# A grouped convolution in the mixed form a second time, and z copied out of PSUM before it is split

## The reference

```python
x = x + conv(x, w0, groups=4, 9 taps, padding 4) + (cond @ c_w0.T + side)[:, :, None]
x = x + agg_w1 @ x + agg_b1[:, :, None]     # agg_w = sum_k att_k W_k, att = softmax of a small MLP of cond
x = x + agg_w2 @ x + agg_b2[:, :, None]
x = x + conv(x, w3, groups=4, 9 taps, padding 4) + (cond @ c_w3.T + side)[:, :, None]
```

## Time and profile before

| | us |
|---|---|
| median of 3 runs | 632.01 (631.92 to 632.13) |
| the profiled execution | 635.33 |
| its span, first to last instruction | 633.5 |
| TensorE busy (share of the span) | 622.8 (98%) |
| VectorE busy | 500.9 (79%) |
| ScalarE busy | 338.2 (53%) |
| GpSimd busy | 272.3 (43%) |
| mean granted TensorE clock | 0.991 |

### The profile page before, as it was taken

One profiled execution on the slowest core, in us unless ns is written; L12 is line 12 of the kernel. 1 busy time (PEld: TensorE's weight loads), 2 busy tenths in 40 slices (PEclk: granted clock), 3 DMA queues, 4 the chain that ended last, 5 costly groups with the idle time before them and its releaser, 6 DMA issues.

```text
span 633.5 us, 26750 instructions
## 1 busy us (share of the span) xinstructions
PE 622.8 (98%) x11938; PEld 506.3 (80%) x11938; DVE 500.9 (79%) x1002; ACT 338.2 (53%) x626; POOL 272.3 (43%) x163
## 2 busy tenths in 40 slices
PE   8999999999999999999999999999999999999995
PEld 6888897777788777889877778777878877788874
DVE  6899777978777887887887887797877788788735
ACT  4665455555455456455456446555545545645534
POOL 4133454354355345355435345435435534534220
PEclk8999999999999999999999999999999999999998
DMA  8066665557765556775555776555776555655515
GB/s 244 24 188 215 203 211 177 204 163 225 232 207 156 190 176 199 232 232 158 173 191 175 232 232 182 158 202 162 223 232 208 155 190 176 201 169 168 161 76 201
DMA packets 50572, 118.84 MB, mean 188 GB/s; under 512 B 5621, under 2 KB 26282, under 8 KB 42714
## 3 DMA queue, kind: packets, MB, share of 16 engines
q1 hardware_dynamic: 49170, 116.04, 58.1%
q0 software_dynamic: 576, 1.26, 0.5%
q10 hardware_dynamic: 776, 0.89, 0.4%
HBM read 35.33 MB, written 33.55 MB: 109 GB/s over the span
## 4 chain that ended last, share of the span: by engine, by line
PE 96%; DMA 2%; DVE 1%; ACT 1%; issue 0%; ACTq 0%; DVEq 0%
PE ps L1068 45%; PE ps L1079 19%; PE ps L1090 16%; PE ps L1214 14%; PE ps L1192 1%; DMA out_sb<-in_L_cond_weight 1%; DMA out_planes<-out_taps 1%; ACT out_sb L740 1%; PE ps L1262 0%; PE ps L1185 0%; DVE out_taps L856 0%; DVE x_in L950 0%; DVE x_hi L993 0%; PE ps L1250 0%; PE ps L1302 0%
## 5 line engine op out<-in xcount | busy, mean ns | idle before, releaser
L513 POOL COPY out_sb<-out_planes 128x2048 f32<-128x2048 f32 x30 | 123.0, 4099 | 187.8 <-issue 162.0
L496 POOL COPY x_full<-x_in 128x2048 f32<-128x2048 f32 x29 | 117.1, 4038 | 113.9 <-DVE x_lo L822 110.1
L846 DVE SCALAR_TENSOR_TENSOR z_lo<-ps,bias_tab,z_hi 128x1024 fp32r<-128x1024 f32 x62 | 76.7, 1279 | 60.7 <-ACT z_hi L649 60.7
L1090 PE MATMUL ps<-x_full,taps_raw 32*32 32x512 f32 x2880 | 102.2, 598 | 0.0
L1068 PEld LDWEIGHTS ps<-z_hi,taps_hi 32*128 32x128 f32 x1488 | 71.0, 183 | 35.4 <-issue 25.1
L1068 PE MATMUL ps<-z_hi,taps_lo 32*128 32x512 f32 x1488 | 96.5, 387 | 0.0
L836 DVE SCALAR_TENSOR_TENSOR y_lo<-ps,bias_tab,y_hi 128x512 fp32r<-128x512 f32 x128 | 87.2, 744 | 10.2 <-ACT y_hi L639 10.2
L1068 PE MATMUL ps<-z_hi,taps_hi 32*128 32x512 f32 x1488 | 94.2, 396 | 0.0
L657 ACT ACTIVATE out_taps<-ps,bias_tab 128x512 f32<-128x512 f32 x62 | 39.3, 685 | 102.2 <-PE ps L1068 102.2
L1068 PE MATMUL ps<-z_lo,taps_hi 32*128 32x512 f32 x1488 | 90.3, 385 | 0.0
L1214 PE MATMUL ps<-y_hi,mix_w 32*128 32x512 f32 x1024 | 88.0, 385 | 0.0
(11 more groups left out here) (158 smaller groups left out, 831.0 us busy)
## 6 DMA issues: line engine op xcount, KB each, us to landing
x_in<-in_x SPq DMA_DIRECT2D x31, 1024.0 KB, 5.3
out_planes<-out_taps SPq DMA_DIRECT2D x122, 256.0 KB, 3.6
out<-out_sb SPq DMA_DIRECT2D x30, 1024.0 KB, 4.6
mix_w<-prod SPq DMA_DIRECT2D x124, 128.0 KB, 4.0
x_in<-in_x SPq DMA_DIRECT2D x2, 512.0 KB, 5.9
out<-out_sb POOLq DMA_DIRECT2D x2, 512.0 KB, 3.5
out<-x_full SPq DMA_DIRECT2D x7, 128.0 KB, 2.9
out_taps<-in_L_cond_weight SPq DMA_DIRECT2D x1, 512.0 KB, 5.8
```

The lines of the kernel that those rows point to most:

```text
L496: pool.tensor_copy(row_order(t, d, x[:, :, home(t, d)]), x_order(t, d, x_in[t.par(d)][:, :])).then_inc(x_planed, 1)
L513: pool.tensor_copy(x_order(t, d, out_sb[t.par(d)][:, :]), row_order(t, d, out_planes[:, :, :]))\
L846: dve.scalar_tensor_tensor(out=z_home(t, 0)[1][:, 2 * h:2 * h + 2, home(t, 0)], in0=ps[:, k:k + 2, :], scalar=bias_tab[:, b, 2 * G:BIAS], ...
L1090: tile = pe.matmul(ps[rows(p), first_bank + g, :], taps_raw[l][rows(g), d - p, :], full[rows(g), d % PH, c:c + S], start=False, stop=(n == ...
```

## The change

Conv3 of tiles 1 to 30 takes the mixed form too. Step t now runs conv0 of tile t with its three tile rounds last, then directly conv3 of tile t - 1 with its three tile rounds first, so that the six stand together, then 6 whole rounds, the product (or, in the last step, the mix), and 12 whole rounds; then the mix. The tile rounds need z unsplit, so ScalarE writes z with its bias from PSUM to a new buffer `z_full` in two halves, fills z_full's edges, and then makes z_hi from z_full in one copy; VectorE makes z_lo from z_full and z_hi in one operation. Conv3's tile rounds wait for z_lo_done and z_full's edges.

The output columns of conv3's weights are now ordered as conv0's, by phase and then by channel, so `relay_out` reads 32 neighbouring partitions for each phase instead of every fourth. The last tile keeps the old order: its taps are made again in conv0's weight buffers (GpSimd clears them after the last conv0, ScalarE and VectorE fill them), and its biases come in a small `bias_last` by four DMA transfers in step 16.

```diff
+FIRST_FULL_Z = 1
+        def full_z(t, d):
+            return not isinstance(t.half, int) or FIRST_FULL_Z <= t.i + d < N - 1
...
-                    sp.dma_start(out_planes[:, p, :], out_taps[p:C:PH, :, :]).then_inc(out_relaid, DMA)
+                    sp.dma_start(out_planes[:, p, :], out_taps[rows(p), :, :]).then_inc(out_relaid, DMA)
...
+            def bias_for_last():
+                pool.wait_ge(bias_tab_done, 3)
+                for p in range(PH):
+                    pool.dma_start(bias_last[p:C:PH, :], bias_tab[rows(p), N - 1, G:2 * G]).then_inc(bias_last_in, DMA)
+            def zero_last_taps():
+                pool.wait_ge(conv0_done, G * N)
+                for w in (taps_hi[0], taps_lo[0]):
+                    pool.memset(w[:, :, :].bitcast(F32), 0.0).then_inc(last_taps_zeroed, 1)
...
-                    for o, i in edges(z):
+                    for o, i in (edges(z, slice(PH - 1, PH), slice(0, 1)) if full_z(t, 0) else edges(z)):
...
+            def whole_z(t):                       # called by high_z(t) where full_z(t, 0)
+                b = t.i
+                for h in range(2):
+                    act.wait_ge(mix_done, PH * b + 2 * h + 2)
+                    k = bank(t, 0) + 2 * h
+                    act.activation(z_full[:, 2 * h:2 * h + 2, home(t, 0)], ps[:, k:k + 2, :], ACT.Identity,
+                                   bias=bias_tab[:, b, 2 * G:BIAS]).then_inc(z_full_done, 1)
+                act.wait_ge(z_full_done, 2 * (b + 1 - FIRST_FULL_Z))
+                for o, i in full_edges(z_full):
+                    last = act.activation(o, i, ACT.Copy)
+                last.then_inc(z_full_edged, 1)
+                act.activation(z_hi[:, :, home(t, 0)], z_full[:, :, home(t, 0)], ACT.Copy).then_inc(z_hi_done, 2)
...
+            def last_taps_high():                 # ScalarE, step 31, ahead of high_z; VectorE has last_taps_low
+                act.wait_ge(last_taps_zeroed, 2)
+                for p in range(PH):
+                    act.activation(last_columns(taps_hi, p), taps_raw[1][:, :, :], ACT.Copy).then_inc(last_taps_hi_done, 1)
...
             def low_z(t):
                 b = t.i
+                if full_z(t, 0):
+                    dve.wait_ge(z_hi_done, 2 * (b + 1))
+                    dve.tensor_tensor(out=z_lo[:, :, home(t, 0)], in0=z_full[:, :, home(t, 0)],
+                                      in1=z_hi[:, :, home(t, 0)].bitcast(F32), op=ALU.subtract).then_inc(z_lo_done, 2)
+                    return
...
+            def conv3_mixed(t, turns, middle):
+                b = t.i - 1
+                order = [(k, d) for k in range(2) for d in WHOLE] + [(2, d) for d in WHOLE]
+                if t.at(2):
+                    pe.wait_ge(taps_raw_step[1], 2)
+                    pe.wait_ge(prod_summed, b + 2)
+                pe.wait_ge(z_lo_done, 2 * (b + 1))
+                pe.wait_ge(z_full_edged, b + 1 - FIRST_FULL_Z)
+                pe.nop(nofuse=True)
+                partial_turns(bank(t, -1), 1, z_full, BLK, first=True)
+                pe.wait_ge(z_edged, b + 1 - PLAIN)
+                whole_turns(bank(t, -1), 1, z_hi, z_lo, order[:turns], BLK)
+                middle()
+                whole_turns(bank(t, -1), 1, z_hi, z_lo, order[turns:], BLK, done=conv3_done)
...
-            LATER = 20
+            LATER = 6
...
-                mid = MID + 4 if t.at(2) else MID if t.at(N - 1) else LATER
-                if t.has(-1):
-                    conv3(t, -1, range(mid))
-                if t.has(1):
-                    product(t, 1)
...
+                elif t.at(N - 1):
+                    conv3_mixed(t, LATER, lambda: mix(t))
+                else:
+                    conv3_mixed(t, LATER, lambda: product(t, 1))
                     mix(t)
```

More of the change, by code:

```diff
@@ L580, in _ @@
                 pool.memset(buf[:, :, ROW - 1:ROW].bitcast(F32), 0.0).then_inc(far_zeroed, 1)
-            for buf in x_full:
+            for buf in x_full + [z_full]:
                 pool.memset(buf[:, :, 0:ROW:ROW - 1], 0.0).then_inc(far_zeroed, 1)
@@ L592, in conditioned_residual_kernel @@
         HALOS = 6
-        FAR = 8
+        FAR = 9
         @block.scalar
@@ L940, in one, with last_taps_low @@
                     low_z(t)
+            def last_taps_low():
+                dve.wait_ge(last_taps_zeroed, 2)
+                for p in range(PH):
+                    dve.wait_ge(last_taps_hi_done, p + 1)
+                    dve.tensor_tensor(out=last_columns(taps_lo, p), in0=taps_raw[1][:, :, :],
+                                      in1=last_columns(taps_hi, p).bitcast(F32), op=ALU.subtract)\
+                       .then_inc(last_taps_lo_done, 1)
             def turn_last(h):
@@ L1078, in whole_turns, with partial_turns @@
                     for g in range(G):
-                        pe.matmul(ps[:, first_bank + g, :], w[rows(g), d, :], a[rows(g), d % PH, c:c + S],
-                                  start=(first and (k, d) == turns[0]), stop=False)
-            def partial_turns(first_bank, l, full, done, step):
+                        tile = pe.matmul(ps[:, first_bank + g, :], w[rows(g), d, :], a[rows(g), d % PH, c:c + S],
+                                         start=(first and (k, d) == turns[0]), stop=(done is not None and (k, d) == turns[-1]))
+                        if done is not None and (k, d) == turns[-1]:
+                            tile.then_inc(done, 1)
+            def partial_turns(first_bank, l, full, step, first=False, done=None):
                 for n in range(PARTIAL):
@@ L1090, in partial_turns @@
                             tile = pe.matmul(ps[rows(p), first_bank + g, :], taps_raw[l][rows(g), d - p, :],
-                                             full[rows(g), d % PH, c:c + S], start=False, stop=(n == PARTIAL - 1))
-                        if n == PARTIAL - 1:
+                                             full[rows(g), d % PH, c:c + S], start=(first and n == 0),
+                                             stop=(done is not None and n == PARTIAL - 1))
+                        if done is not None and n == PARTIAL - 1:
                             tile.then_inc(done, 1)
@@ L1232, in one @@
                     mix(t)
-                    return
-                mid = MID + 4 if t.at(2) else MID if t.at(N - 1) else LATER
-                if t.has(-1):
-                    conv3(t, -1, range(mid))
-                if t.has(1):
-                    product(t, 1)
-                if t.at(N - 1):
-                    mix(t)
-                if t.has(-1):
-                    conv3(t, -1, range(mid, TURNS))
-                if t.has(0) and not t.at(N - 1):
+                elif t.at(N - 1):
+                    conv3_mixed(t, LATER, lambda: mix(t))
+                else:
+                    conv3_mixed(t, LATER, lambda: product(t, 1))
                     mix(t)
```

58 lines of the change are left out of this document (39 added, 19 removed).

## The result

The change makes the kernel 22% slower: 773.49 us (762.19 to 774.46, 3 runs) against 632.01, a ratio of 1.2146 (95% interval 1.1994 to 1.2299). The forecast was 724 us in a range of 697 to 762: the sign was right, the size was not.

The account below looks back on a forecast made before the run. TensorE's work and an equally long chain through ScalarE and VectorE (18.82 us a step) were taken to bound the kernel. 632.0 + 72 (loop) + 0.6 (end) + 19 (clock) = 724 us, range 697 to 762.

Parts of the forecast that it names:

- Chain from Z to z_lo: From Z, the start of the x_hi matmuls, z_lo ends after 7.31 us instead of 3.87, 3.45 us later.
- y_lo 7.97 behind z_lo: VectorE's matrix steps start at z_lo's end, so y_lo ends 7.97 us after it, at Z + 15.3.
- The product waits some 3.2 us: TensorE reaches the product at Z + 12.2 and waits some 3.2 us for y_lo in every step.
- TensorE alone would need 18.0: Conv3 gives up 18 rounds for three tile rounds, gaining 0.8 us; if nothing else bound, the step would be 18.0.
- Conv3's tile rounds lose 0.1 at most: TensorE reaches conv3's tile rounds at about Z + 7.4, so waiting for z_lo_done loses about 0.1 us at most.
- 705 if the clock holds: Whole kernel: 632.0 + 72 for the loop + 0.6 for the last step = 704.6 us, without clock falls.
- I take the fall in one step of four: Waits before the product lower the clock, 2.6 us per fall, in one step of four: 0.65 x 29 = 19 us.
- rival C: The chain, and a clock fall in nearly every step: 780 us, range 745 to 790; chance 16%.
- rival A: The chain as worked out, and the clock holds: 705 us, bounds 698 to 711; chance 32%.
- Step 2, 2.0 us: Step 2 had 14 rounds behind the product, not 16, so it wins less back and pays about 2.0 us.
- The end, +0.6: In the last step last_conv waits some 1.2 us, against 0.6 us of conv3 saved: +0.6 us.
- The transfers of 32 neighbouring partitions, priced at nothing: Output transfers out_planes take 3.6 us and have 18.8; they would have to take over 10 us to be felt.

Follow-up runs that it names:

- the run with six zeros: The changed kernel with 6 matmuls of zero weights added into conv3's open sums ahead of each product: 703.08 us, ratio 1.1111.
- the second profile: Profile of the changed kernel run once more, unchanged, for its spread; its times were 770.57, 776.23, 751.77 and 771.68 us.
- z's way alone: The changed kernel with z still through z_full, but conv3 in its old form of 36 whole rounds, LATER = 20: 759.42 us, ratio 1.2018.
- the fastest version: Changed kernel with z_hi and z_lo straight from PSUM, ScalarE emptying three of conv3's four banks, step 1's x_lo edge copies ahead of z_full: 612.23 us, ratio 0.9684.

## Why the forecast was right in sign and wrong in size

- **Chain from Z to z_lo, 7.31 us forecast, 3.45 later than before:** 7.20 measured. The edge copies were 0.61 (forecast 0.62), z_hi 1.90 (1.93), z_lo 2.29 (2.29). Right.
- **y_lo 7.97 behind z_lo, at Z + 15.3:** Z + 15.17. Right, and so was the reason: VectorE's matrix steps and ScalarE's split of them stand between.
- **The product waits some 3.2 us:** its matmul idles 2.77, its weight load 3.20. Right. The step without a fall, 21.3 forecast, was 21.33 and 21.29 in steps 2 and 3, whose matrices are not split, and from product to product 21.03 behind them. The term that was too dear is the 0.3 between y_lo and the product: 0.06 measured. So 28 steps cost 2.2 us each, not 2.5, and the loop 64, not 72.
- **TensorE alone would need 18.0:** 17.97, in the run with three banks on ScalarE.
- **Conv3's tile rounds lose 0.1 at most:** they lost 1.0 once, in step 3, and nothing in a later step.
- **705 if the clock holds:** 703.08 in the run with six zeros, in which it holds through the loop. That it comes so near is partly luck: its steps were 0.25 us shorter than forecast, 7 us in all, its step 2 and its end together some 6 us longer.
- **The clock. This is the step that failed: "I take the fall in one step of four: 0.65 x 29 = 19 us."** The size of one fall was near, 2.86 us against 2.6: it begins 0.7 us ahead of the product, where the forecast put it in mid-wait, 1.6 ahead. Its frequency was wrong: 27 of 29 steps had one, 26 of them in full, 76 us in all instead of 19. That is rival C (780, with 745 to 790), which had 16%. The measured time is 632 + 64 + 76 and the 2.6 us at the end: the falls came out 57 us dearer than forecast, the chain 8 us cheaper.
- **What the forecast had for and against it.** For one fall in four steps it had no row, only two bounds. With the idle time before the product as it is (2.8 us), the loop had a fall of 6.8 us in each step from the second fall on; with 0.77 us of it left, and also with none, there was no fall from 200 to 600 us and the work around it was the same. So the idle time is shown as the cause. The dense work on both sides, rival A's reason, did not keep the clock up, except in step 4 of the second profile. Rival C's reason, that the steps are all alike, is not shown either: that step 4 had the full wait and no fall, and with z's way alone (another conv3, waits of 2.3 and 0.5 us) one in five of like steps had none. C was right in its number; why the falls come in every step once they have begun stays open.
- The Trainium skill ("TensorE: Matmul & The Clock Gate", section "HAM oscillation — how this bites in real kernels") describes this: a loop that falls back to 1.2 GHz in each wait and pays again each turn. This trace agrees, with 6.8 us at 0.50 in each of 26 steps. The waits of the page's loop are for a DMA, about 3 to 5 us; the one here is 2.8 us and for VectorE.
- **Step 2, 2.0 us:** 1.75 (19.58 before, 21.33 after), but not where it was forecast. Nothing was lost at the product; 1.36 us went where conv0 waited for the edge copies of x_lo, which in that step stand behind z's longer work in ScalarE's program (L643 in the waits above). A queue position that the forecast had not followed.
- **The end, +0.6:** last_conv waited 1.35 us for x_lo (forecast 1.2) and began 19.41 us behind the last x_hi matmuls, 18.70 before: +0.7. A pause of 1.2 us within it, which the profile puts down to issue, was not forecast; from the last x_hi matmuls of the loop to the end it is 2.6 us more than before. The remade taps were not wholly hidden: ScalarE's four taps (from 748.34) were followed at once by its next work at 750.41, 0.83 us behind the start of the last mix matmuls (749.58), where it is 0.48 before (612.51 and 612.99). About 0.35 us of last_conv's wait is theirs.
- **The transfers of 32 neighbouring partitions, priced at nothing:** they land in 4.7 us instead of 3.6, and TensorE never waits for them; the fastest version has them too. Whether the partitions are the cause was not tested: the load of x, which was not changed, also takes longer in the changed kernel, 7.3 us against 5.3.

What stays open is what would predict whether a fall comes and how long it is; the idle time alone does not. The run with VectorE's matrices first waited 1.64 us in each step before the tile rounds and had no fall from 200 to 500 us and one behind; the one with GpSimd's copy held back waited 2.1 us before conv0 and had a fall only now and then. Their waits stand elsewhere in the step. These are points, not a curve.

## What to carry to other kernels

Before a matmul saving is booked, follow the hand-over that feeds the next stage and read its slack: here TensorE was 98% busy and yet a second chain of the same length ran beside it, so 3.3 us more on that chain cost 2.2 us a step, and of the TensorE work saved only the four rounds behind the product (0.9 us), which stand on the chain, won anything. Price an idle time of TensorE that returns in every step twice, once as the wait and once as the clock, and give the case of a fall in every step a real chance. Filling the wait with useful rounds, or giving the work in front to an idle engine, wins back both. If an extra copy of a result is needed, make it behind the copies that the chain waits for, and look again at who is last: the gain came in full only when the next queue, conv3's evacuation, was relieved too.

## What the runs showed of the hardware

- An operation of VectorE with two SBUF inputs, and a cast from SBUF to SBUF, stood still until GpSimd's running copy of 128x2048 had ended: 3.02 against 0.35 us, 2.22 against 0.23. y_lo, with one input in PSUM, took 2.73 us with a GpSimd copy beside it (that copy starts at 316.85 in the change) and 2.71 with none (at 26.76). The Trainium skill ("SBUF — State Buffer", section "Who interferes with whom") says that such a VectorE instruction contends with a GpSimd instruction that reads SBUF, that a cast may too, and that whoever comes second is blocked for all of the other's instruction. The traces agree: the two ended 0.15 and 0.08 us after the copy.
- With a wait of 2.8 us in each step, the granted clock was halved for 6.8 us in 26 steps that follow each other (25 in the second profile); the same wait in an early step brought a fall of 3.4 us in one execution and none in another. With 1.65 us of matmuls by zeros in the wait, no fall came from 200 to 600 us.
- Where a fall begins goes with its length: those of 6.8 us in the changed kernel's loop begin ahead of the product; those of 3.4 us, one in each profile of it and all of z's way alone from 200 us on, begin behind it.
